# Filtered messages in a graph-network kernel: rings of three steps instead of two, and the weights' steps spread evenly over the messages' steps

## The reference

```python
filt = jax.nn.silu(rbf @ Wf1 + bf1) @ Wf2 + bf2
msg = x[col] * filt
agg = jax.ops.segment_sum(msg, row, num_segments=x.shape[0])
```

```python
a_in = jax.ops.segment_sum(feat_in[src] * iw[:, None], dst, num_segments=N)
a_out = jax.ops.segment_sum(feat_out[dst] * ow[:, None], src, num_segments=N)
```

## Time and profile before

| | us |
|---|---|
| median of 3 runs | 7822.07 |
| lowest and highest | 7807.66, 7825.48 |
| profiled execution, device time | 7872.61 |
| its span, first to last instruction | 7870.9 |

### The profile page before, as it was taken

One profiled execution on the slowest core, in us unless ns is written; L12 is line 12 of the kernel. 1 busy time (PEld: TensorE's weight loads), 2 busy tenths in 40 slices (PEclk: granted clock), 3 DMA queues, 4 the chain that ended last, 5 costly groups with the idle time before them and its releaser, 6 DMA issues.

```text
span 7870.9 us, 88068 instructions
## 1 busy us (share of the span) xinstructions
PE 5294.4 (67%) x23224; PEld 3511.6 (45%) x23225; DVE 4742.8 (60%) x6614; ACT 2203.1 (28%) x4590; POOL 2850.9 (36%) x4180
## 2 busy tenths in 40 slices
PE   8523444699944448883388866666666799994838
PEld 4312233487822126763233325555555645483213
DVE  9862222475521127879999987777777610026987
ACT  6411111243311115522255541112211310012524
POOL 0277777517767771000000005666676000000000
PEclk9995666799955559996699987777777799995968
DMA  9940111259976663336422325656566223304775
GB/s 253 274 106 11 37 39 40 73 167 292 292 234 215 211 213 134 129 107 175 134 67 67 83 72 187 194 193 197 195 201 189 45 97 132 132 30 123 205 195 150
DMA packets 717764, 1158.60 MB, mean 147 GB/s; under 512 B 273349, under 2 KB 487003, under 8 KB 702994
## 3 DMA queue, kind: packets, MB, share of 16 engines
q1 hardware_dynamic: 374010, 608.16, 26.7%
q10 hardware_dynamic: 228664, 291.39, 11.1%
q0 software_dynamic: 114784, 255.38, 10.2%
HBM read 670.62 MB, written 483.97 MB: 147 GB/s over the span
## 4 chain that ended last, share of the span: by engine, by line
PE 34%; DVE 28%; issue 17%; DMA 9%; another core or an unknown queue 8%; POOL 2%; ACT 1%; SPq 1%; DVEq 1%; ACTq 0%; POOLq 0%
PE psall L1497 10%; PE psall L1470 7%; DVE arena L2167 7%; DVE arena L2135 4%; PE psall L1563 3%; DMA arena<-weights_out 3%; PE psall L1630 3%; DMA arena<-weights_in 2%; DVE arena L2362 2%; DVE arena L2219 2%; DVE arena L2160 2%; DMA arena<-table_x,arena 2%; POOL arena L959 2%; PE psall L1575 1%
## 5 line engine op out<-in xcount | busy, mean ns | idle before, releaser
L959 POOL DMA_INDIRECT arena<-table_x,arena x856 | 955.5, 1116 | 2182.1 <-DMA arena<-slots_by_src 1849.8
L1497 PE MATMUL psall<-arena 128*128 128x250 f32 x2880 | 864.1, 447 | 468.3 <-issue 426.0
L1540 PE MATMUL psall<-arena 128*65 128x312 f32 (+3 forms) x3000 | 948.5, 440 | 217.8 <-DVE arena L2167 217.6
L1470 PE MATMUL psall<-shared_w,arena 128*128 128x256 f32 x3264 | 855.2, 419 | 308.2 <-DVE arena L2079 279.0
L923 POOL DMA_INDIRECT slots_by_block_pair<-arena x806 | 797.9, 990 | 562.1 <-DVE arena L1944 314.5
L1116 ACT ACTIVATE arena<-psall 128x250 f32<-128x250 f32 (+2 forms) x1002 | 327.0, 367 | 2145.5 <-PE psall L1497 767.0
L1497 PEld LDWEIGHTS psall<-arena 128*128 128x128 f32 x2880 | 581.1, 217 | 751.8 <-issue 700.0
L948 POOL DMA_INDIRECT slots_by_src<-arena,pos_s x806 | 783.0, 971 | 268.6 <-issue 171.8
L1470 PEld LDWEIGHTS psall<-shared_w,arena 128*128 128x128 f32 x3264 | 664.2, 210 | 427.9 <-DVE arena L2079 271.7
L1563 PE MATMUL psall<-arena 128*125 128x256 f32 x1712 | 585.5, 515 | 345.5 <-DVE arena L2219 241.4
L2079 DVE TENSOR_TENSOR arena<-psall,shared_w 128x512 f32<-128x512 f32 x408 | 280.2, 690 | 820.0 <-remote 510.8
(11 more groups left out here) (323 smaller groups left out, 7496.6 us busy)
## 6 DMA issues: line engine op xcount, KB each, us to landing
arena<-counts SPq DMA_DIRECT2D x375, 312.5 KB, 3.4
arena<-slots_by_src SPq DMA_DIRECT2D x107, 1040.0 KB
filters<-arena ACTq DMA_DIRECT2D x204, 520.0 KB
slots_by_src<-shared_on SPq DMA_DIRECT2D x8, 9230.0 KB
arena<-filters SPq DMA_DIRECT2D x138, 520.0 KB
counts<-arena ACTq DMA_DIRECT2D x125, 312.5 KB
weights_in<-arena ACTq DMA_DIRECT2D x125, 312.5 KB
arena<-counts ACTq DMA_DIRECT2D x25, 1562.5 KB
```

What stands on the lines that cost most here:

```text
L959: G.indirect_dma_start(hg[:, f % 2, j, :], None, t_x1, bass.IndirectOffsetOnAxis(ap=pay_s[:, f % 2, j, S_IDX:S_IDX + 1].bitcast(I32), axis ...
L1470: last = MM(to, hidT[:, sl % 2, c, j * LANES:(j + 1) * LANES], wf2[:, c, :], start=(c == 0), stop=(c == 1))
L1497: MM(psall[:, bass.ds(half_at(words[k], j), 2 * P)], ohs[:, sl, TG * k + j, :], ohw[:, sl, TG * k + j, :, :].rearrange("p a k -> p (a k)") ...
L1540: last = MM(ps[gat_bank(n, wn, h_, c)][0:F + 1, 0:z - a], rows, g["e1"][:, q % RE, a:z], start=(b == 0), stop=(b == NT - 1))
```

## The change

Records and features get a third slot each (`EDGE_RING = 3`), placed behind the stores' staging tile in the arena. Load, gather and message of step f use slot f % 3 and wait for step f-3; the third load has no wait any more and is issued with the first two. The one-hot tiles of the messages keep two slots, as do those of the weights.

The 120 weights' steps are no longer one to a turn. `weight_steps(i)` gives turn i the steps from 120·i/108 to 120·(i+1)/108, rounded down. Turns 0 to 107 have one each, except turns 8, 17, 26 and so on to 107, twelve in all, which have two; turns 108 to 110 have none. The loops have 111 turns on DVE and 110 on PE. Two scores' DMAs early in the program add to one semaphore instead of two (`as_in`, `as_more`), and the wait for them is a single one.

```diff
+EDGE_RING = 3
...
-        pay_s = view(o_pay, LANES, 2 * F_T * S_REC).rearrange("p (s j c) -> p s j c", s=2, j=F_T)
-        hg = view(o_hg, LANES, 2 * F_T * D).rearrange("p (s j f) -> p s j f", s=2, j=F_T)
...
+        o_last = o_ws + 3 * PAIRS * LANES
+        pay_s = [view(o_, LANES, F_T * S_REC).rearrange("p (j c) -> p j c", j=F_T)
+                 for o_ in (o_pay, o_pay + F_T * S_REC, o_last)]
+        hg = [view(o_, LANES, F_T * D).rearrange("p (j f) -> p j f", j=F_T)
+              for o_ in (o_hg, o_hg + F_T * D, o_last + F_T * S_REC)]
...
+        def weight_steps(i):
+
+            return range(min(W_STEPS, W_STEPS * i // (F_STEPS + 1)), min(W_STEPS, W_STEPS * (i + 1) // (F_STEPS + 1)))
...
             def edge_load(f):
-                if f >= 2:
-                    sp.wait_ge(s["e_onehot"], f - 1)
-                    sp.wait_ge(s["e_msg"], f - 1)
-                sp.dma_start(pay_s[:, f % 2, :, :], vs[:, F_T * f:F_T * (f + 1), :]).then_inc(pay_in[f % 2], 16)
-
-            edge_load(0)
-            edge_load(1)
+                if f >= EDGE_RING:
+                    sp.wait_ge(s["e_onehot"], f - EDGE_RING + 1)
+                    sp.wait_ge(s["e_msg"], f - EDGE_RING + 1)
+                sp.dma_start(pay_s[f % EDGE_RING], vs[:, F_T * f:F_T * (f + 1), :]).then_inc(pay_in[f % EDGE_RING], 16)
+
+            for f in range(EDGE_RING):
+                edge_load(f)
...
-                    if f >= 2 and j % TS_G == 0:
-                        pool.wait_ge(s["e_sum"], F_G * (f - 2) + j // TS_G + 1)
+                    if f >= EDGE_RING and j % TS_G == 0:
+                        pool.wait_ge(s["e_sum"], F_G * (f - EDGE_RING) + j // TS_G + 1)
...
-            for i in range(max(W_STEPS + 1, F_STEPS + AHEAD)):
-                if 0 <= i - AHEAD < F_STEPS:
+            for i in range(F_STEPS + AHEAD):
+                if i >= AHEAD:
                     edge_sums(i - AHEAD)
-                if 1 <= i <= W_STEPS:
-                    weight_sums(i - 1)
+                for n in weight_steps(i - 1) if i else ():
+                    weight_sums(n)
...
-            for i in range(max(W_STEPS, F_STEPS + AHEAD + 1)):
+            for i in range(F_STEPS + AHEAD + 1):
                 f = i - AHEAD
                 if 0 <= f < F_STEPS:
                     messages(f)
                 if 0 <= f - 1 < F_STEPS:
                     adds(f - 1)
-                if i < W_STEPS:
-                    weight_onehots(i)
-                if 0 <= f + 1 < F_STEPS:
+                for n in weight_steps(i):
+                    weight_onehots(n)
+                    if n == weight_steps(i)[0] and 0 <= f + 1 < F_STEPS:
+                        edge_onehots(f + 1)
+                    weighed(n)
+                if not weight_steps(i) and 0 <= f + 1 < F_STEPS:
                     edge_onehots(f + 1)
-                if i < W_STEPS:
-                    weighed(i)
```

More of the change, by code:

```diff
@@ L450, in gnn_kernel @@
         ringed = [sem(f"ringed{s}") for s in range(SLOTS)]
-        pay_in, feat_in = ([sem(f"{n}{s}") for s in range(2)] for n in ("pay_in", "feat_in"))
+        pay_in, feat_in = ([sem(f"{n}{s}") for s in range(EDGE_RING)] for n in ("pay_in", "feat_in"))
+        def weight_steps(i):
+            return range(min(W_STEPS, W_STEPS * i // (F_STEPS + 1)), min(W_STEPS, W_STEPS * (i + 1) // (F_STEPS + 1)))
         def sums_at(n):
@@ L473, in gnn_kernel @@
                f_turned f_tcopied f_hidden f_act f_mm f_out f_aux f_step
-             cb_pay cb_oh  cb_mm cb_free cb_ev as_more
+             cb_pay cb_oh  cb_mm cb_free cb_ev
               x_tr x_mask x_max
@@ L819, in _ @@
             sp.dma_start(ends_w, d_last).then_inc(s["tab_in"], 16)
-            for f in range(2, F_STEPS):
+            for f in range(EDGE_RING, F_STEPS):
                 edge_load(f)
@@ L954, in _ @@
             for f in range(F_STEPS):
[L955 removed]
+                r = f % EDGE_RING
+                pool.wait_ge(pay_in[r], 16 * (f // EDGE_RING + 1))
                 for j in range(F_T):
[L957 to L961 removed]
+                    if f >= EDGE_RING and j % TS_G == 0:
+                        pool.wait_ge(s["e_sum"], F_G * (f - EDGE_RING) + j // TS_G + 1)
+                    G.indirect_dma_start(hg[r][:, j, :], None, t_x1,
+                                         bass.IndirectOffsetOnAxis(ap=pay_s[r][:, j, S_IDX:S_IDX + 1].bitcast(I32),
+                                                                   axis=0)).then_inc(feat_in[r], 16)
         @block.scalar
@@ L1562, in edge_sums @@
                     for j in range(TS_G):
-                        last = MM(sums_at(n), oh[:, f % 2, TS_G * g + j, :], hg[:, f % 2, TS_G * g + j, :],
+                        last = MM(sums_at(n), oh[:, f % 2, TS_G * g + j, :], hg[f % EDGE_RING][:, TS_G * g + j, :],
                                   start=(j == 0), stop=(j == TS_G - 1))
@@ L2125, in _ @@
                 pair_onehots(n)
-            dve.wait_ge(s["as_in"], 32)
-            dve.wait_ge(s["as_more"], 32)
+            dve.wait_ge(s["as_in"], 64)
             for i in range(NT):
@@ L2209, in edge_onehots @@
             def edge_onehots(f):
-                dve.wait_ge(pay_in[f % 2], 16 * (f // 2 + 1))
+                dve.wait_ge(pay_in[f % EDGE_RING], 16 * (f // EDGE_RING + 1))
                 if f >= 2:
@@ L2213, in edge_onehots @@
                 V.tensor_tensor(oh[:, f % 2, :, :], iota_p[:, 0:P].unsqueeze(1).to_broadcast([LANES, F_T, P]),
-                                pay_s[:, f % 2, :, S_LO:S_LO + 1].to_broadcast([LANES, F_T, P]), ALU.is_equal)\
+                                pay_s[f % EDGE_RING][:, :, S_LO:S_LO + 1].to_broadcast([LANES, F_T, P]), ALU.is_equal)\
                     .then_inc(s["e_onehot"], 1)
             def messages(f):
-                dve.wait_ge(feat_in[f % 2], 16 * F_T * (f // 2 + 1))
-                V.tensor_tensor(hg[:, f % 2, :, :], hg[:, f % 2, :, :], pay_s[:, f % 2, :, 0:D], ALU.mult)\
+                r = f % EDGE_RING
+                dve.wait_ge(feat_in[r], 16 * F_T * (f // EDGE_RING + 1))
+                V.tensor_tensor(hg[r], hg[r], pay_s[r][:, :, 0:D], ALU.mult)\
                     .then_inc(s["e_msg"], 1)
@@ L2356, in maxima3 @@
             def maxima3(n, blocks):
-                dve.wait_ge(s["as_in"], 16 * (2 + n))
+                dve.wait_ge(s["as_in"], 16 * (4 + n))
                 for i in blocks:
```

3 lines of the change are left out of this document (2 added, 1 removed).

## The result

The changed kernel takes 7906.9 us (median of 4, 7887.21 to 7912.75) beside 7818.85 us of the kernel before on the same chip: a ratio of 1.0114 [1.0097, 1.0131], slower by 88 us where +41 was forecast. The time lies within the range; the move is twice its size.

What follows compares the result with a forecast made beforehand. No engine was full: waits set the step, counted on DVE, the fullest. Terms -104 + 4 + 30 - 3 + 34 + 94 - 14 = +41 us on 7872.6, carried as a ratio to 7822.07, gave 7863 us; range 7765 to 7945.

Steps and rivals of the forecast that it cites:

- Features: DVE's wait for gathered features ahead of the messages: the ring of three removes all of it, -104 us.
- The third load: At the stage's start, the third load stands ahead of the weights' records in SP's queue and delays it, +4 us.
- The tail: Weights' steps behind the last message: DVE's work there is not saved, only its small waits go, -3 us.
- Place B: First weights' one-hots behind a double turn: DVE waits for PE, 7.0 us plus 1.5 for lateness, 11 times, 94 us.
- Place A: Second weights' one-hots of a double turn: DVE waits for PE, 1.3 us plus 1.5 for lateness, 12 times, 34 us.
- third rival: Much faster: late signals come from the ring of two and shrink too, -30 to -100 us, near 7725; chance 0.05.
- The returned wait: Ahead of the weights' one-hots: part of the removed feature wait comes back as wait for PE's late signals, +30 us.
- signs of being wrong: Short or absent waits behind double turns, features still making DVE wait, or shrinking waits outside the double turns.
- The faster rival: Double turns cost only PE's products and no feature wait returns: -24 to -60 us, 7798 to 7762; chance 0.20.
- 0.4 us: Estimated signal tail of a PE weights' step with 12 products and 12 increments, from the skill's formula.
- POOL as the bound: POOL's gathers set the stage and half the feature wait stays: 7915 us; shares the 0.11 chance of slower still.
- slower still: Slower than forecast, by POOL or later signals at double turns, the latter +170 us, 7991; chance 0.11.

Runs made afterwards that it cites:

- changed_third: The changed kernel, unedited, run beside the kernel before on a chip that showed no late signals: ratio 0.9871 [0.9855, 0.9887].
- ring3_alone: Rings of three as in the changed kernel, but weights' steps one to a turn with ten turns behind the last message: ratio 0.9948 against the kernel before.
- before_grouped: The kernel before, with PE signalling once for four products of the weights instead of on each: ratio 1.001 against the kernel before.
- set 1: Follow-up runs on one chip with late signals, each compared with the kernel before, which takes 7821 us there.
- after_grouped: The changed kernel, with PE signalling once for four products of the weights instead of on each: ratio 1.0102 against the kernel before.

## Why the prediction was right and wrong

*Features, -104*: right, -101. *The third load, +4*: right (1.04 / 0.283 is 3.7, not 3.8): DVE's wait ahead of its first weights' step goes from 35.9 to 38.6 us. *The tail, -3, and what is behind the last message*: right. It starts 1492 us after the stage (6193.16 - 4701.1), where 6220 - 4738 = 1482 was forecast, and 14.7 us lie behind it:

```profile
6193.16 2.29 DVE L2231 TENSOR_TENSOR arena<-arena 128x2048 f32<-128x2048 f32 x1
...
6203.97 0.42 DVE L2244 TENSOR_TENSOR arena<-arena,psall 125x256 f32 x1 [6.21 <-PE psall L1575]
...
6207.87 0.42 DVE L2035 COPY tT<-psall 128x250 f32<-128x250 f32 x1 [1.11 <-PE psall L1428]
```

*Place B, 11 × (7.0 + 1.5) = 94*: right in both parts. Without late signals it is 75.5 us, 6.9 each (changed_third), with them 97.3, another 2.0 each; the same kernel without gathers has 75.5 on a chip with late signals too.

*Place A, 12 × (1.3 + 1.5) = 34*: **this is the step that failed**: "the bounds are nothing and 6.6, the longest wait seen; I take 1.5". PE's products cost 0.6 us each there (changed_third, 6.6 us); the signals' lateness cost (160.9 - 6.6) / 12 = 12.9 us each. The longest wait seen was no bound. A wait lasted over at most four gathers of POOL with rings of two, and over up to thirteen with rings of three. The third slot, of eight gathers, is what lets POOL go on while DVE stands; ring3_alone, with up to ten, shows that the ring does it without double turns. That a wait ends because POOL has run out of slots is my reading of these counts. I had the earlier trace rows with POOL's pauses and the earlier trace rows with the late signals, and did not lay the two timelines side by side. The sentence under the third rival, "nothing in the change touches PE's signals", was wrong for the same reason.

*The returned wait, +30, on top of 133*: wrong the other way, and one of the signs of being wrong that I had named. Outside A and B 26.9 us were left where 133 + 30 - 14 = 149 was forecast. The ring is not what took them: with it alone they are 146 us, against 141 in before_grouped. It is the double turns that did. After each long wait at A POOL has used up its records and pauses (15.66 us in the timeline above), so the next turns are free of late signals. That these pauses are the reason is argued, not shown. The two errors, +127 and -122, almost cancel, and the forecast's 275 us at L2249's counterpart met 284 by luck. With 19 us more ahead of the adds, the waits give -101 + 151 - 3 + 19 = +66; the stage grew by 53.7.

*The base*: the sum was made against an execution 50 us above its median and carried over as a ratio. These 50 us lay ahead of the stage and not in it: in before_grouped, profiled in an execution of 7818 us, the stage starts 53 us sooner and takes 1450.5 us, against 1453.1. The 34 us that the two first profiles leave open are at least in part such scatter between executions. In set 1 the stage of after_grouped is 71.1 us longer than that of before_grouped, where the medians differ by 77.5; the changed kernel's stage, with this form of it, took 1499.5 to 1521.6 us in three profiles.

*The faster rival* ("PE's signals are in time where it counts", -24 to -60) came true on the chips without late signals, with -90 us: A 7 against its 16, B 76 against its 77. Why it is 30 to 66 us better than that can't be said, as no profile of the kernel before was taken there.

*Of PE's signals* the Trainium skill (TensorE: Matmul & The Clock Gate, "The cost: per-tile semaphore tail") gives the number of increments as the cost. No run here bears the 0.4 us out: twelve or three increments make no difference. The records of the semaphore lie 13 to 15 ns behind the product where no signal is late, and the last of the turn shown stands 18.3 us behind.

*POOL as the bound* did not come: with 246 us of waits for records it has time to spare, and its slow gathers (100 took over 1.5 us in this profile, 2.7 us on the median) left features only 3.4 us late in all. (The sum of the case *slower still* comes to +174 us, not +170, by its own terms.)

## What to carry to other kernels

Lay the waiting engine's timeline over those of all others before a wait seen today is taken as the bound of a new one; here most of the long waits ended when POOL paused. Give waits on PE's results a turn of slack where POOL issues indirect DMAs in long runs: PE's order (weights' steps first) took the changed kernel from 1.0114, or 1.0102 with fewer signals, to 0.9901 [0.9871, 0.9931] and, in another set, 0.9848 [0.9774, 0.9922], the best among the full kernels on the chips with late signals. The deeper ring alone, with its turn of slack, gained 0.5% there, and lost 1% once the double turns took the slack. A change whose sign hangs on it should be timed on more than one chip.

## What was not expected of the hardware

- PE's signals arrived up to 19.6 us after the product's end while POOL issued 9 to 13 indirect DMAs, one each 1.25 us, and in seven of ten places came 1.4 to 3.4 us after the last of them. The semaphore's own records show it: with POOL idle 12 to 15 ns behind the product, beside gathers microseconds behind it, in the same execution. With POOL idle and the same ring and double turns no wait was over 7.5 us, all for products. What inside the chip holds them is open.
- Three sets (and the first runs) showed this and four did not, with the same program: 7692 to 7821 us for the kernel before against 6869 to 6899, 11 to 14% apart. Early in the program (to 2200 us) DVE's waits named remote at one line come to 430 to 579 us on the first kind, and on the second they are absent. There the same line waits for PE alone, 214.5 us in changed_third, 1.8 us at most. The mean granted clock of the sets' runs differs too, 0.78 to 0.83 against 0.83 to 0.87. No run parts it from the late signals, and why the chips differ is open.
